# A graph attention kernel on one core: gathers in pairs, first gathers by source dots, copies and dots of turned rows at later steps

## What is computed

```python
def _gat_conv(x, src, dst, W, a_src, a_dst, b, n_nodes):
    h = x @ W
    s = h @ a_src
    d = h @ a_dst
    e = s[src] + d[dst]
    e = jnp.where(e > 0, e, NEG_SLOPE * e)
    e_max = jax.ops.segment_max(e, dst, num_segments=n_nodes)
    e_max = jnp.where(jnp.isfinite(e_max), e_max, 0.0)
    w = jnp.exp(e - e_max[dst])
    denom = jax.ops.segment_sum(w, dst, num_segments=n_nodes)
    alpha = w / (denom[dst] + EPS)
    out = jax.ops.segment_sum(alpha[:, None] * h[src], dst, num_segments=n_nodes)
    return out + b
# src, dst: the edges and one loop per node; three layers:
for m in range(Ws.shape[0]):
    x = x + jax.nn.sigmoid(_gat_conv(x, src, dst, Ws[m], att_src[m], att_dst[m], bias[m], n))
```

## Time and profile before

| | us |
|---|---|
| median of three runs (7064.27 to 7081.72) | 7068.47 |
| the profiled execution | 6998.82 |
| its span, first to last instruction | 6997.0 |
| PE busy in it | 5196.8 (74%) |
| DVE busy | 4413.0 (63%) |
| POOL busy | 3585.5 (51%) |
| ACT busy | 3451.3 (49%) |

### The profile page before, as it was taken

One profiled execution on the slowest core, in us unless ns is written; L12 is line 12 of the kernel. 1 busy time (PEld: TensorE's weight loads), 2 busy tenths in 40 slices (PEclk: granted clock), 3 DMA queues, 4 the chain that ended last, 5 costly groups with the idle time before them and its releaser, 6 DMA issues. The chain is left out here.

```text
span 6997.0 us, 99999 instructions
## 1 busy us (share of the span) xinstructions
PE 5196.8 (74%) x23702; PEld 3069.4 (44%) x23702; DVE 4413.0 (63%) x12021; ACT 3451.3 (49%) x7591; POOL 3585.5 (51%) x3533
## 2 busy tenths in 40 slices
PE   3899999999946567547663767698889976666665
PEld 2566566666521334323332334465556643333332
DVE  5888888888746777657765889455445533333333
ACT  2788888888757345435542556323223322222222
POOL 2444444444224554366626552466566646676665
PEclk9999999999978678767876778799999988888887
DMA  9988887776556455445545676566567753333332
GB/s 173 266 273 288 275 269 242 239 240 233 191 179 207 141 157 163 127 130 166 165 138 148 220 225 219 164 183 185 181 196 231 227 156 102 98 108 106 102 100 70
DMA packets 934341, 1274.02 MB, mean 182 GB/s; under 512 B 273590, under 2 KB 423799, under 8 KB 927411
## 3 DMA queue, kind: packets, MB, share of 16 engines
q1 hardware_dynamic: 721002, 1063.92, 47.0%
q0 software_dynamic: 112896, 202.19, 12.1%
q10 hardware_dynamic: 100016, 3.20, 1.2%
HBM read 623.49 MB, written 654.07 MB: 183 GB/s over the span
## 5 line engine op out<-in xcount | busy, mean ns | idle before, releaser
L1726 POOL DMA_INDIRECT n_xs<-table,look x1176 | 1184.0, 1007 | 738.8 <-issue 317.1
L1867 DVE TENSOR_TENSOR_SCAN n_dT<-n_km,n_dT,bank 128x512 f32<-128x512 uint8 x291 | 372.2, 1279 | 1356.0 <-DMA g_kn<-keep_floats 618.7
L1441 POOL DMA_INDIRECT g_xs<-table,look x784 | 786.4, 1003 | 759.2 <-POOLq L206 270.9
L628 POOL DMA_INDIRECT p_rows<-in_x_dram,dst_ix x392 | 383.1, 977 | 595.2 <-DMA raw_rows<-p_rows 340.1
L636 POOL DMA_INDIRECT table<-slot_pair,map_ix x392 | 395.5, 1009 | 465.1 <-ACT n_sg L744 253.1
L1737 POOL DMA_INDIRECT out_dram<-n_xn,n_row_of x392 | 442.2, 1128 | 340.2 <-ACT n_xn L1849 212.8
L1827 ACT ACTIVATE n_eT<-bank,edge_b 128x512 f32<-128x512 f32 x294 | 202.1, 687 | 808.1 <-PE bank L1769 482.1
L672 PE MATMUL bank<-n_xT,gat_w 128*128 128x512 f32 (+1 forms) x1176 | 558.9, 612 | 51.6 <-ACT n_xT L736 26.8
L691 PE MATMUL bank<-n_zT,wn 128*128 128x512 f32 (+1 forms) x1176 | 540.7, 595 | 16.9 <-issue 10.2
L1820 ACT ACTIVATE n_sT<-bank 128x512 f32<-128x512 f32 x294 | 175.6, 597 | 723.6 <-DMA dots<-g_dt 488.4
L1555 ACT ACTIVATE g_xw<-g_xs,g_cols 128x128 f32<-128x128 f32 x1176 | 371.0, 387 | 175.4 <-issue 81.8
(11 more groups left out here) (271 smaller groups left out, 12390.5 us busy)
## 6 DMA issues: line engine op xcount, KB each, us to landing
table<-n_ro SPq DMA_DIRECT2D x768, 256.0 KB
g_gb<-decays SPq DMA_DIRECT2D x294, 256.0 KB
n_xd<-table SPq DMA_DIRECT2D x294, 256.0 KB
table<-g_xn SPq DMA_DIRECT2D x196, 256.0 KB
g_xo<-table SPq DMA_DIRECT2D x196, 256.0 KB
edge_feats<-n_eT SPq DMA_DIRECT2D x196, 256.0 KB
table<-n_xn SPq DMA_DIRECT2D x196, 256.0 KB
n_ea<-edge_feats SPq DMA_DIRECT2D x196, 256.0 KB
```

The costliest lines, as they stand in the source:

```text
L628: q.indirect_dma_start(out=edge_rows[e % UX][:, u, :], out_offset=None, in_=x, in_offset=bass.IndirectOffsetOnAxis(ap=dst_ix[:, t:t + 1], ...
L1441: q.indirect_dma_start(out=xs[g % XR][:, u, :], out_offset=None, in_=tables[l], in_offset=bass.IndirectOffsetOnAxis(ap=src_ix[:, t:t + 1] ...
L1726: q.indirect_dma_start(out=xs.buffers[g % UE][:, u, :], out_offset=None, in_=tables[L], in_offset=bass.IndirectOffsetOnAxis(ap=look[:, t, ...
L1867: V.tensor_tensor_scan(in_order(dT[g][:, :]), kept(g), in_order(flat_banks[1]), 0.0 if begins(g) else carry(dT[g.before(1)]), ALU.mult, AL ...
```

## The change

Three things, all in `gat_pass`.

1. `gather` has two more waits. For groups 4 to `XR` - 1, group g waits until the source dots of group g - 1 are done. In pass 0 no such group is gathered by the pass, so this concerns groups 4 to 19 of passes 1 and 2. And between the second and the third transfer of a group it waits until ACT has gated group g - XR - 5, which stands in the same step of ACT as the scaling for which the first pair waits, behind it.
2. In passes 0 and 1 `copy_back` moves from lag 23 to 24, `dot` from 24 to 25, `copy_dots` from 24 to 26, `store_dots` from 25 to 27.
3. No instruction of an engine is added or taken away but waits.

```diff
@@ sync
-                                else [(23, store_rows), (25, store_dots)]))
+                                else [(23, store_rows), (27, store_dots)]))
@@ gpsimd, gather(g)
                             ready(q, scaled, g - XR + 1)
                             if l == 0:
                                 ready(q, looked, g - XR + 1)
-                            for u in range(U):
+                            if 4 <= g < XR:
+                                q.wait_ge(sdot, g)
+                            for u in range(U):
+                                if u == U // 2:
+                                    ready(q, tanh, g - XR - 4)
                                 t = g * U + u
                                 q.indirect_dma_start(
@@ tensor
-                             + ([(19, join_rows)] if last_layer else [(23, turn_back), (24, dot)]))
+                             + ([(19, join_rows)] if last_layer else [(23, turn_back), (25, dot)]))
@@ scalar
-                             + ([(30, normalise)] if last_layer else [(23, copy_back), (24, copy_dots)]))
+                             + ([(30, normalise)] if last_layer else [(24, copy_back), (26, copy_dots)]))
```

## The result

The change made the kernel slower, by less than half a percent. The profiled execution after has a span of 7094.0 us, 97 more than before, but 29 of these lie ahead of the first gather of pass 0 and 8 behind the last turn of pass 2, where the code is the same. A single execution is that uneven, and the one before, 6998.82 us, was shorter than each of the 20 timed ones (7051.61 and up); the passes themselves are the better measure: pass 0 takes 571.5 us from its first gather to its last turn (before 576.4), pass 1 740.6 (697.7) and pass 2 788.1 (774.1).

A forecast was written before the change was run, and what follows sets the result against it. No engine was taken as full in passes 0 and 1, signals being late beside unbroken gathers; DVE was close to the bound in pass 2. -30 - 16 + 4 + 0 = -42 us gave 7026 us, range 6942 to 7110.

The forecast's parts named there:

- The first turn: Opening of pass 1: PE's first turn of scaled rows near 92 us from the first gather instead of 128.
- A paced group at 7.4 us: Groups 4 to 19 of passes 1 and 2, each waiting for the previous dots: 7.4 us a group against 5.0.
- the sum of -30: Gain from pacing first gathers by dots: group 20's dots 11.2 us earlier in pass 1, 18.5 in pass 2.
- The step that failed: Openings of passes 1 and 2: pacing's gain read at group 20's dots, -30 us; POOL's lateness named as next, without a price.
- Its own sign of being wrong: Passes 1 and 2: forecast wrong if the time between groups 20 and 28 grows by more than the start gave.
- The slower rival: Behind group 19: eight owed groups gathered at once, 40 us unbroken, DVE standing; +26 us, 7095 us; chance of slower 0.22.
- Its other half: First softmax chain keeps 54 us and starts 7 us later, gathers late too: +14 us a pass, 7100; within slower's 0.22.
- The rival of no change: Group cost stays 6.3 to 6.6 us, later copies give nothing, POOL's missing time costs 24 us: about 7066 us; chance 0.23.
- The much faster rival: Stalls of passes 0 and 1 mostly go: about -130 + 4 us, 6942 us; chance 0.12.
- Part 2, -16 us: Passes 0 and 1, later copies and dots of turned rows: longer rows of gathers save 0.12 us a group, -16 us.
- +4 us at a pass end: Ends of passes 0 and 1: one more dot outstanding, one round of 1.78 us, twice, +4 us in all.
- Part 3, 0: Second pair of a group's gathers waits for ACT's gate: between -43 and +43 us in pass 2, taken as 0.

The follow-up runs named there:

- debt_slow: The full change, but behind group 19 the wait for dots goes on to group 43, let loose by one group in three: 1.0126 of the kernel before, 7058.35 us.
- pace_to_12: The kernel before, with only groups 4 to 12 of passes 1 and 2 waiting for the dots of the group before: ratio 1.0036.
- the ring of 16: The kernel before with a ring of 16 groups instead of 20 in passes 1 and 2, on the chip where before takes 6186.63 us: ratio 1.0003.

## Why the prediction was wrong

- **The first turn** of pass 1 was to come 92 us from the first gather: it came at 94.8, and 98.3 in pass 2. Nearly right, though the softmax chain was taken at 10.8 us and took 25.4: it was hidden under the pacing, as said.
- **A paced group at 7.4 us**: 7.8 from group 4 to 12 ((3018.56 - 2955.92) / 8) and 8.3 from 12 to 19 (58.07 / 7), since by then the turns have begun and DVE has other work. So the dots of group 20 came 156.8 us from the first gather, where 146 was forecast and 157.4 measured before; in pass 2 164.6 and 164.2. The 11.2 and 18.5 us, the sum of -30, are not there at all: the price of a paced group was forecast too low.
- **The step that failed** is the one that set the gain of part 1 at the dots of group 20 and took the pipeline as unchanged from there. "Eight groups of ring that used to be filled ahead are not" stood in the text with no price. The runs give it: 9.75 groups at 6.6 us, 64 us against the 33 saved, so that part 1 costs 42 us in pass 1 where -11 was forecast, and 41 in pass 2 where -18.5 was. The prediction had 6.4 to 6.6 us a group from its first rows and never applied them to the groups it moved. Its own sign of being wrong came: from the dots of group 20 to those of group 27 it is 83.2 us, where it was 46.9.
- **The slower rival** had the sign, the place and the time (7095 us against 7102.55). Its mechanism is in the trace: 48 gathers behind group 19, DVE standing in the second half and 7 us beyond; dots of group 27 at 240.0 us from the first gather, where it said 221 and before had 204.3. Its reason was half right: debt_slow and pace_to_12 show that the length of the row doesn't decide the loss. The time matched by luck: part 3 took back in pass 2 some of what the debt cost beyond the estimate of 22 us.
- **Its other half**, that the row isn't what makes signals late and the chain keeps its 54 us, is refuted for this chip: 25.4 us with pacing. The Trainium skill's rule (SBUF — State Buffer, Who interferes with whom), that TensorE and ScalarE never wait for GpSimd, is one on ports of the SBUF. The chip of 6187 us, where the chain beside gathers took 18.4 us, does not speak against it. On the chips of 7000 us it was no guide to this outcome: 18 and 23 us passed between a TensorE record and the VectorE instruction that reads its result while gathers ran. That these are waits for a port is not shown; it is the signal that is late.
- **The rival of no change** was nearest in its reason: a group has much the same price whatever the row, part 2 gives nothing, and POOL's missing time eats part 1. It priced that at 24 us for both passes, where the groups moved cost 64 in pass 1 alone. **The much faster rival** needed the stalls of passes 0 and 1 to go, and they only moved from ACT's copy to PE's turn.
- **Part 2, -16 us**: alone +37, with part 3 nothing. Where the waits would go was right (PE's turn, ACT's gate), and that they would be shorter there was wrong. +4 us at a pass end was right for one end (4.2), but it was the sum of both ends, which took +8.4.
- **Part 3, 0**: -20 us alone, of which pass 2 shows 35. The text had the term, -43 if a stall ends sooner, and set it to nothing by DVE's share of 83%. In part 3's pass 2 DVE goes on to 89% (460.91 of 515 us in 3760:4275), so 83% was not full. That row:

```profile
3760.00:4275.00 515.00, 373.26 (x1412) 207.33 (x1413) 460.91 (x1824) 280.43 (x744) 303.37 (x300) 0.84 0.73 230
```

In sum the traces have part 1 at +42 and +41 us, part 3 at -35 in pass 2, the pass ends at +8, which is +56; the timed runs say +26 for the whole. The difference is open, and the trace before was a short execution.

## What to carry to other kernels

When work of an engine is held back in an opening and so moved into a running pipeline, price it at what it costs there, beside everything else, not at what it costs alone: an earlier first result was worth nothing or less here, since the same gathers were still owed. Then look at the other end: a ring that is filled far ahead ends in a tail with no gather in it, and a lead held short gave the only gain of 1% here. It gave nothing where GpSimd or VectorE was full, since their work stays the same. A share of 83% busy is no proof that an engine is full; see what ends its waits.

## What was not expected of the hardware

The same kernel takes 6187 us on one chip and 6988 to 7096 on the others. On the former the waits looked at are short beside POOL's gathers (first chain 18.4 us instead of 54.2, a group at 5.3 us instead of 6.5). On the latter a result of PE was taken up by DVE up to 23 us after PE's record ends, and the waits of the steady part stay with a quarter of the bytes or a quarter of the rows. Where nothing is gathered the chips are alike: the first chain of pass 0 takes 10.8 us on both, and from the turn of group 87 to that of group 97 of pass 1, in the tail, it is 35.12 us in the kernel before (from 3566.41) and 35.12 us in the ring of 16 on the faster chip (from 3230.97). What makes the difference beside gathers is not shown. The full change and its parts were not run on the faster chip, so what it does there is not known. A lead held short, worth 0.5 to 1% on the others, made no difference there; nor did the size of the ring, which was not tried on the others.
